# Cross-attention and a routed FFN on one core: values laid out by the host in six tiles of 125 keys, and the first batch's loads in another order

## The reference, cut to what matters

```
def _L0_xattn_ref(query, key):                 # query (8,224,2048), key = ctx_4096 (8,750,2048)
    a = jnp.einsum('bqd,bkd->bqk', query, key)
    e = jax.nn.softmax(a, axis=-1)
    return jnp.einsum('bqk,bkd->bqd', e, key)
x = x + _L0_xattn_ref(_layernorm(x), ctx_4096)
x = x + _L0_ffn_ref(_layernorm(x), ...)        # base 2048x2048 product, 16 low-rank experts, top 2
```

## Time and profile before

| | |
|---|---|
| median of 3 runs | 1351.94 us (1350.43 to 1354.08) |
| the profiled execution | 1354.39 us, span from first to last instruction 1352.6 us, mean granted TensorE clock 0.996 |
| PE busy | 1327.3 us of the span (98%) |
| DVE, ACT, POOL busy | 974.7, 601.2 and 322.5 us |
| data moved by DMA | 345.67 MB |

### The profile page before, as it was taken

One profiled execution on the slowest core, in us unless ns is written; L12 is line 12 of the kernel. 1 busy time (PEld: TensorE's weight loads), 2 busy tenths in 40 slices (PEclk: granted clock), 3 DMA queues, 4 the chain that ended last, 5 costly groups with the idle time before them and its releaser, 6 DMA issues.

```text
span 1352.6 us, 16784 instructions
## 1 busy us (share of the span) xinstructions
PE 1327.3 (98%) x6543; PEld 1081.0 (80%) x6543; DVE 974.7 (72%) x1254; ACT 601.2 (44%) x768; POOL 322.5 (24%) x229
## 2 busy tenths in 40 slices
PE   7799999999999999999999999999999999999998
PEld 5578788887878788887888888888788888888887
DVE  5698888889798888879475467777677555465554
ACT  3356554645546464546321367877686211111110
POOL 0003012130302112120615723354442111111110
PEclk9899999999999999999999999999999999999999
DMA  9976968878796977769657598999995977878775
GB/s 326 315 258 215 294 242 242 269 251 271 227 304 212 287 259 248 246 227 194 201 161 211 176 296 288 321 324 310 315 250 192 322 255 242 281 250 263 253 260 164
DMA packets 159359, 345.67 MB, mean 256 GB/s; under 512 B 51696, under 2 KB 68080, under 8 KB 145520
## 3 DMA queue, kind: packets, MB, share of 16 engines
q1 hardware_dynamic: 140688, 277.06, 64.5%
q0 software_dynamic: 10528, 52.85, 12.6%
q10 hardware_dynamic: 8064, 14.68, 3.1%
HBM read 260.87 MB, written 99.41 MB: 266 GB/s over the span
## 4 chain that ended last, share of the span: by engine, by line
PE 75%; DVE 12%; DMA 5%; ACT 3%; POOL 3%; issue 2%; SPq 0%; DVEq 0%; POOLq 0%; ACTq 0%
PE scores L937 12%; PE scores L939 12%; PE scores L938 12%; PE scores L906 6%; PE scores L908 6%; PE scores L907 6%; PE scores L789 4%; PE scores L791 3%; PE scores L790 3%; DVE ctxT_l L1287 3%; PE work L973 2%; PE work L974 2%; DMA y_scratch<-y_out,yrow_i 2%; DVE raw_l L1297 2%; POOL hs_scratch L1830 2%
## 5 line engine op out<-in xcount | busy, mean ns | idle before, releaser
L937 PE MATMUL scores<-w_h,a_h 128*128 128x512 f32 x896 | 352.0, 393 | 0.0
L939 PE MATMUL scores<-w_h,a_l 128*128 128x512 f32 x896 | 350.9, 392 | 0.0
L938 PE MATMUL scores<-w_l,a_h 128*128 128x512 f32 x896 | 350.6, 391 | 0.0
L1159 ACT ACTIVATE a_h<-a_in 128x512 fp32r<-128x512 f32 x148 | 83.6, 622 | 313.4 <-DMA a_in<-xT_scratch 211.3
L939 PEld LDWEIGHTS scores<-w_h,a_l 128*128 128x128 f32 x896 | 168.4, 188 | 37.5
L937 PEld LDWEIGHTS scores<-w_h,a_h 128*128 128x128 f32 x896 | 168.3, 188 | 37.5 <-DVE w_l L1584 0.3
L938 PEld LDWEIGHTS scores<-w_l,a_h 128*128 128x128 f32 x896 | 168.5, 188 | 37.1
L1593 DVE TENSOR_TENSOR a_l<-a_in,a_h 128x512 fp32r<-128x512 f32 x148 | 106.0, 763 | 115.3 <-ACT a_h L1159 111.8
L789 PE MATMUL scores<-ctxT_h,nT_h 128*112 128x494 f32 (+1 forms) x512 | 174.3, 340 | 7.8 <-DVE nT_l L1485 7.2
L1067 ACT ACTIVATE val_h<-raw_in 128x512 fp32r<-128x512 f32 x192 | 120.2, 629 | 127.6 <-PE scores L908 127.6
L791 PE MATMUL scores<-ctxT_h,nT_l 128*112 128x494 f32 (+1 forms) x512 | 171.5, 335 | 0.0
(11 more groups left out here) (168 smaller groups left out, 1936.6 us busy)
## 6 DMA issues: line engine op xcount, KB each, us to landing
ctxT_in<-in_ctxT_dram SPq DMA_DIRECT2D x63, 750.0 KB, 4.7
raw_in<-in_ctx_dram SPq DMA_DIRECT2D x32, 1280.0 KB
a_in<-xT_scratch SPq DMA_DIRECT2D x37, 1024.0 KB
w_in<-in_wT_dram SPq DMA_DIRECT2D x32, 512.0 KB, 6.7
y_add<-y_scratch SPq DMA_DIRECT2D x56, 256.0 KB, 6.2
late_y<-y_scratch SPq DMA_DIRECT2D x56, 256.0 KB, 6.0
nT_in<-in_xT_dram SPq DMA_DIRECT2D x7, 1792.0 KB, 10.1
res<-x_scratch SPq DMA_DIRECT2D x42, 256.0 KB
```

Of the source, the lines that this page charges most:

```text
L937: pe.matmul(o, ah, wh, start=(k == 0), stop=False)
L938: pe.matmul(o, ah, wl, start=False, stop=False)
L939: last = pe.matmul(o, al, wh, start=False, stop=(k == KD - 1))
```

## The change

The host lays the values out as `[batch, chunk, partition, tile, column]` with key = tile x 125 + partition, so that one chunk of one batch is one transfer of 125 partitions with 12,288 contiguous bytes each. All six key tiles have 125 rows (`KT = LK // NT`), so `rows_of`, the 110-row remainder, the padding of `prob` and its memset fall away, the transposes take 125 columns, and high and low parts and matmuls of the values run on 125 partitions. `raw_loaded` counts one transfer of 16 for each chunk and batch where it was two. In the first batch chunk 1 is loaded right behind chunk 0, chunk 2 behind `ctxT` piece 6 (ahead of piece 7), and chunk 3 ahead of `arT`.

```diff
-    LK = ctx.shape[1]
+    LK = ctxT.shape[-1]
-    FULL = LK // P
-    REST = LK - FULL * P
+    KT = LK // NT
...
-            prob = sb("prob", [QT, NQ, NT * P], F32, first)
+            prob = sb("prob", [QT, NQ, LK], F32, first)
...
             def load_raw(b, c):
-                cols = slice(c * BANK, (c + 1) * BANK)
-                sp.dma_start(raw_in[:, c, 0:FULL, :],
-                             ctx[b, 0:FULL * P, cols].rearrange("(t p) d -> p t d", p=P)).then_inc(raw_loaded[c], 16)
-                sp.dma_start(raw_in[0:REST, c, FULL, :], ctx[b, FULL * P:LK, cols]).then_inc(raw_loaded[c], 16)
+                sp.dma_start(raw_in[0:KT, c, :, :], ctx[b, c]).then_inc(raw_loaded[c], 16)
...
                     load_ctxT(b, j)
                     if first and j == LR:
                         load_row(0)
-                    if first and j == LR + 1:
-                        load_raw(0, 1)
+                    if first and j == NPC - 2:
+                        load_raw(0, 2)
...
                     if first:
-                        load_raw(0, 2)
+                        load_raw(0, 3)
                         sp.dma_start(ar_in[:, :, :], arT).then_inc(ar_loaded, 16)
-                        load_raw(0, 3)
                         load_row(1)
...
             load_raw(0, 0)
+            load_raw(0, 1)
             one(0, "first")
...
-                        last = pe.transpose(work[:, slot, at:at + QT],
-                                            prob[:, q, t * P:(t + 1) * P], ident[0:QT, 0:QT])
+                        last = pe.transpose(work[0:KT, slot, at:at + QT],
+                                            prob[:, q, t * KT:(t + 1) * KT], ident[0:QT, 0:QT])
...
-                        eh, el = eT_h[0:used, q, t, :], eT_l[0:used, q, t, :]
-                        vh, vl = val_h[0:used, e % NR, :], raw[0:used, c, t, :]
+                        eh, el = eT_h[0:KT, q, t, :], eT_l[0:KT, q, t, :]
+                        vh, vl = val_h[0:KT, e % NR, :], raw[0:KT, c, t, :]
...
-                    act.wait_ge(raw_loaded[c], b * 32 + 32)
-                used = rows_of(t)
-                act.activation(val_h[0:used, e % NR, :], raw_in[0:used, c, t, :],
+                    act.wait_ge(raw_loaded[c], b * 16 + 16)
+                act.activation(val_h[0:KT, e % NR, :], raw_in[0:KT, c, t, :],
                                ACT.Copy).then_inc(val_high, 1)
...
-            dve.memset(prob[:, :, LK:NT * P], 0.0).then_inc(consts_ready, 1)
...
+    laid["ctx_4096"] = ctx.reshape(nb, -(-lk // 128), -1, d // 512, 512).transpose(0, 3, 2, 1, 4)
```

More of the change, by code:

```diff
@@ L78, in xattn_ffn_kernel @@
     NT = -(-LK // P)
-    FULL = LK // P
-    REST = LK - FULL * P
+    KT = LK // NT
     CH = D // BANK
     RE = R + E
-    assert LQ == NQ * QT and D == CH * BANK and RE <= P and 2 * R == P
+    assert LK == NT * KT and LQ == NQ * QT and D == CH * BANK and RE <= P and 2 * R == P
     T = NB * LQ
@@ L468, in xT_count @@
             return 16 * sum(len(pieces_of(b)) for b in range(batches))
-        def rows_of(t):
-            return P if t < FULL else REST
         X2T_TAIL_AT = (3, 6, 9, 12)
@@ L1037, in high @@
                 act.wait_ge(filled, job_no(stage, b, name, n) + 1)
-                src = place(stage, name, n).rearrange("p (k c) -> p k c", k=cols)[:, :, 0:width]
+                rows = out.shape[0]
+                src = place(stage, name, n)[0:rows, :].rearrange("p (k c) -> p k c", k=cols)[:, :, 0:width]
                 act.activation(out, src, ACT.Copy).then_inc(high_done, 1)
@@ L1121, in one @@
                 for q in range(NQ):
-                    high(stage, b, "eT", q, eT_h[:, q, :, :].rearrange("p (k i) c -> p k (i c)", k=2), 2, 3 * QT)
+                    high(stage, b, "eT", q, eT_h[0:KT, q, :, :].rearrange("p (k i) c -> p k (i c)", k=2), 2, 3 * QT)
                 for e in range(NR, CH * NT):
@@ L1281, in low @@
                 dve.wait_ge(high_done, act_no(stage, b, name, n) + 1)
-                src = place(stage, name, n).rearrange("p (k c) -> p k c", k=cols)[:, :, 0:width]
+                rows = low_part.shape[0]
+                src = place(stage, name, n)[0:rows, :].rearrange("p (k c) -> p k c", k=cols)[:, :, 0:width]
                 dve.tensor_tensor(low_part, src, as_f32(high_part), ALU.subtract).then_inc(drained, 1)
@@ L1295, in value_low @@
                 dve.wait_ge(val_high, b * (CH * NT) + e + 1)
-                used = rows_of(t)
-                dve.tensor_tensor(raw[0:used, c, t, :], raw_in[0:used, c, t, :], as_f32(val_h[0:used, e % NR, :]),
+                dve.tensor_tensor(raw[0:KT, c, t, :], raw_in[0:KT, c, t, :], as_f32(val_h[0:KT, e % NR, :]),
                                   ALU.subtract).then_inc(val_ready, 1)
@@ L1452, in run_route @@
                     dve.wait_ge(row_ids, 2)
-                    dve.wait_ge(consts_ready, 1 + E)
+                    dve.wait_ge(consts_ready, E)
                 for n in range(lo, hi):
@@ L1543, in one @@
                 for q in range(NQ):
-                    three = lambda tile: tile[:, q, :, :].rearrange("p (k i) c -> p k (i c)", k=2)
+                    three = lambda tile: tile[0:KT, q, :, :].rearrange("p (k i) c -> p k (i c)", k=2)
                     low(stage, b, "eT", q, three(eT_h), three(eT_l), 2, 3 * QT)
```

## The result

The changed kernel takes **1525.8 us** (median of 5 runs, 1521.9 to 1531.9); the kernel before, on the same chip, 1353.0 (5 runs, 1350.4 to 1357.4). The ratio is 1.128, 95% interval 1.124 to 1.131: 172.8 us slower. The forecast was 1453, range 1400 to 1515: the sign and the five engines were right, the size was not.

A forecast was written before the change was run, and what follows sets the result against it. The opening was taken as bound by the DMA queue, other batches by PE with transfers hidden. Terms of 20.4 + 8 + 72.6 = 101 us on 1354.4, which stands 2.45 over the median, gave 1453 us, range 1400 to 1515.

The forecast's parts named there:

- Low parts, PE, SP: nothing: Value low parts, matmuls, transposes and SP's issues: no change in cost, booked as zero.
- Five engines, the same for every chunk: Value chunk loads: 125 rows run on five DMA engines, 25 rows each, always the same five; chance 0.83 at 26 to 27 GB/s.
- The line ahead of piece 4: Mid batches: chunks and stores queue ahead of `ctxT` piece 4, which lands at 425.8; PE stands 9.9 us.
- The price of a chunk, 11.5 us: Value chunk on five engines: 11.5 us, from the pace of loads with long runs; ends 11.3 and 17.6.
- The upper end that I carried, 17.6 us from the x rows: Value chunk on five engines at the 17.5 GB/s an engine of the 112-row x loads: 17.6 us.
- The clock: Behind each PE pause: eleven matmuls run slower at the lower clock, 2.2 us a stall.
- The stall is paid once a batch: Mid batches: pieces 5 to 7 follow faster than PE uses them, so 12.1 us a batch with the clock, six times.
- Into batch 1: Step into batch 1: no row stores to wait behind, but the opening's backlog is ahead; between 4 and 12, taken as 8 us.
- The opening: First batch: scores of piece 7 start at 66.9 instead of 48.70; 18.2 us, and 2.2 for the clock.
- the load doesn't spread: Value chunks spread over all 16 engines: same time, 1355 us, chance 0.06; or faster opening, 1347 us, chance 0.04.
- isn't at 17.5 GB/s alone: Value chunks on five engines at the pace of the x loads, 17.6 us a chunk: 1600 us, chance 0.04.
- doesn't change engines: Value chunks on five engines, but others for each chunk, so they run side by side: 1360 us, chance 0.03.

The follow-up runs named there:

- e1: Changed kernel with each value chunk padded by the host from 125 to 128 partitions, new load order kept: 1352.3 us, ratio 0.999.
- e5: Changed kernel with each value chunk padded by the host to 126 partitions, for fourteen engines: 1363.1 us, ratio 1.009.
- e14: Kernel with values padded to 128 partitions, but chunk 0 of each batch loaded by 125 rows: 1375.3 us, ratio 1.016.
- e7: Changed kernel with values padded to 128 partitions, old first-batch load order, and x rows padded from 112 to 128: 1349.0 us, ratio 0.996.
- e13: Changed kernel with ACT instead of SP issuing the value chunks of every batch after the first: 1486.0 us, ratio 1.098.

## Why the prediction was right about the mechanism and wrong about the size

*Low parts, PE, SP: nothing.* Right. The low parts at 125 rows, by the costliest groups, against the earlier trace rows:

```profile
L1289 DVE TENSOR_TENSOR raw_l<-raw_in,val_h 125x512 fp32r<-125x512 f32 x192 | 153.1, 824 | 23.4 <-ACT val_h L1059 23.3
```

153.1 us in all, where before it was 133.3 + 21.9.

*Five engines, the same for every chunk.* Right: 5 small packets, a share of 0.32; and if the five had changed from chunk to chunk, there would be no line to wait in. By the rule of the Trainium skill that the prediction cites ("DMA: Bandwidth & Descriptors", "Why a DMA increments its semaphore by 16 and not by 1"), 128 rows on 16 engines and 126 on 14 would both have ended the line; e1 and the later batches of e5 agree.

*The line ahead of piece 4.* Right in kind. ACT waits for the piece, PE for ACT and DVE, in every batch; in e14, with one slow chunk in the line, PE waits for no piece in the middle batches.

*The price of a chunk, 11.5 us. This is the step that failed.* It came from rows in which one kind of load runs alone, and I applied it to a line in company. "A chunk runs on five engines" was taken to mean that the other eleven go about their work undisturbed. They don't, and neither do the five: the pieces issued behind the chunks run ahead on eleven engines, and while they do, all engines move 13.4 to 14.3 GB/s instead of 26.4. A piece thus slows the very chunk that its own share on the five engines is queued behind. By its 125 packets of 12,288 bytes in the trace, chunk 1 of the batch above runs from 217.5 to 229.5, ahead of the pieces: 12.1 us. Chunk 2 runs beside them, from 229.3 to 247.4: 18.1 us where 11.5 stood. From chunk 0's issue to piece 4's landing the forecast had 425.8 - 376.9 = 48.9 us; measured, 253.99 - 198.08 = 55.9. These 7.0 us more are the whole error in the stall, 16.95 instead of 9.9, and chunk 2 alone gives 6.6. The upper end that I carried, 17.6 us from the x rows, may be another face of the same effect, and I dismissed it as "another cut of the partitions". The cut is what makes the x rows slow (e7).

*The clock.* Right: between landmarks 2 and 3 the kernel lost 18.8 us, of which 16.95 are the stall; 1.8 are left for the lower clock behind it, where 2.2 were forecast.

*Later steps.* "The stall is paid once a batch" held, but the batches don't lose the same: 15.1 to 21.4 us a step. *Into batch 1* 16.2 for 8: the row stores are absent, as forecast; chunk 0, issued at 104.0, sends its first packet at 109.3, behind the opening's backlog, and chunk 2 takes 18.6 us beside the pieces, again not 11.5.

*The opening.* 35.4 for 20.4, the same term again. The scores of piece 7 were to start at 66.9; PE's timeline:

```profile
53.96 0.75 PE L782 MATMUL scores<-ctxT_h,nT_h 128*112 128x494 f32 x1 [23.47 <-DVE nT_l L1477]
...
82.46 0.75 PE L782 MATMUL scores<-ctxT_h,nT_h 128*112 128x494 f32 x1 [13.32 <-DVE nT_l L1477]
```

82.46 against 48.70 before: 33.8 us, 15.6 more than forecast. Two chunks on five engines meet x rows and pieces at the half pace until 37 us (226, 223 GB/s above) and are through at 47.2, where 37.0 was forecast. Chunk 2 then meets the second block of x rows, which stands behind piece 7 in SP's order and which the sum had left out, and more pieces: it runs from 57.3 to 75.8, 18.5 us for 11.5.

*The sum, with the terms that were measured:* 35.4 + 16.2 + (18.8 + 21.4 + 21.3 + 19.8 + 19.5 + 15.1 = 116) = 167.6, where 20.4 + 8 + 72.6 = 101 stood. The rivals all fell: the load doesn't spread (5 small packets), isn't at 17.5 GB/s alone (26.4), and doesn't change engines.

**What stays open.** That loads of 125, 126 and 112 rows are slow beside others or alone, and that the pace comes back with 128, is shown by the changed kernel, e5, e1 and e7; *why*, at which end, and why such a load slows loads beside it and stores hardly, is not. The Trainium skill, "SBUF — State Buffer", section "Door 1: The DMA port swizzle (why `[64,N]` ≈ `[32,N]`)", has DMA reach the memory by 16 ports, each for two groups of four partitions. Engines with 25, 9 or 7 rows would not be cut along these groups as eight rows an engine are, and could meet at a port; no run here shows which port a packet used. How much of e13's remaining 130 us is the row stores' turn-taking, how much the half pace and how much the plain load of the five engines was not separated.

## What to carry to other kernels

Before a load is cut to the exact number of rows that hold data, work out into how many engines that number divides, and look at what queues behind it: padding 125 rows to 128 cost 2.4% of the values' bytes and took away the whole loss of 12.8%. A mean DMA share (78% before) says nothing once a transfer sits on a few engines, because a transfer that is spread over all of them ends with its slowest share. And a price read from a transfer that runs alone is a lower bound for one that runs in company: look for a row with the same company, or carry twice the price as the other end.

## What the runs showed of the hardware that was not expected

- A load into 125 partitions halves the pace of the loads that run beside it, and its own: 13.4 to 14.3 GB/s a busy engine for 26.4. Beside x2 stores it was 23.3. Loads into 126 partitions, with nothing beside them, ran at 24.9 in one stretch and 16.7 in another.
- A load into 112 partitions moves 280 GB/s on 16 engines; a stretch with the same rows in 128 partitions, padded, 430.
- Two queues on one engine take turns by the packet, whatever its size: 125 of 12,288 bytes (and 5 small ones) and 130 of some 384 in the same 12 us.
- An issue isn't free: SP stood 11.3 to 30.9 us in the issues of a row store where chunks of 125 rows were under way, 7.4 in the kernel before. It also stood 13.7 us in the issue of one piece in the opening (at 30.52).
